# An expert stage whose VectorE order and whose release of one PSUM bank are changed

## The reference

```
def _expert(x, g, b, W1, b1, W2, b2, Wo, bo):     # D = 128, H = 512
    x = _layernorm(x, g, b)
    x1 = x @ W1 + b1
    x2 = jnp.clip(x @ W2 + b2, -20.0, 20.0)
    hidden = jnp.clip(x1 * (x2 * jax.nn.sigmoid(x2)), -10000.0, 10000.0)
    return jnp.clip(hidden @ Wo + bo, -10000.0, 10000.0)
```

## Time and profile before

| | |
|---|---|
| median of 3 runs | 2611.97 us |
| the profiled execution's own time | 2612.07 us |
| its span | 2610.4 us |
| PE busy | 2346.8 us (90%) |
| DVE busy | 2235.7 us (86%) |
| ACT busy | 1657.2 us (63%) |
| POOL busy | 1498.2 us (57%) |
| mean granted TensorE clock | 0.954 |

### The profile page before, as it was taken

The page is one execution under the profiler, slowest core; times in us unless marked ns, Lnnn a source line. Parts: engine busy times, 40 slices in busy tenths (PEclk is TensorE's granted clock), DMA queues, the critical chain, the costliest instruction groups (busy, mean ns, idle before and its releaser), DMA issues. The chain is left out here.

```text
span 2610.4 us, 44164 instructions
## 1 busy us (share of the span) xinstructions
PE 2346.8 (90%) x15048; PEld 1785.9 (68%) x15048; DVE 2235.7 (86%) x4680; ACT 1657.2 (63%) x2873; POOL 1498.2 (57%) x1073
## 2 busy tenths in 40 slices
PE   5995699927999999999999999999999999939994
PEld 3553588715777777777777777777777777628883
DVE  6666477759999999999999999999999999847775
ACT  2464233336777777787877778787778877623333
POOL 0145344415666666667668766666866766734442
PEclk8997799958999999999999999999999999969997
DMA  8721466563454345334422342233323332025555
GB/s 203 212 69 41 139 191 189 153 153 97 98 128 100 89 99 131 92 87 103 97 61 70 84 94 71 61 76 83 95 63 76 77 87 49 14 68 184 187 181 159
DMA packets 171280, 281.11 MB, mean 108 GB/s; under 512 B 33292, under 2 KB 124818, under 8 KB 171056
## 3 DMA queue, kind: packets, MB, share of 16 engines
q1 hardware_dynamic: 161392, 259.31, 38.7%
q0 software_dynamic: 9664, 18.97, 2.1%
HBM read 118.15 MB, written 63.31 MB: 70 GB/s over the span
## 5 line engine op out<-in xcount | busy, mean ns | idle before, releaser
L2334 POOL TENSOR_TENSOR b_prob<-b_prob,b_weight 128x1024 f32<-128x1024 f32 x512 | 958.8, 1904 | 504.5 <-DVE b_weight L2292 503.4
L2262 DVE TENSOR_REDUCE b_bmax<-b_score 128x16 f32<-128x1024 f32 x512 | 620.9, 1213 | 42.5 <-PE b_score L2113 27.4
L2214 ACT ACTIVATE b_prob<-b_score,b_neg_m 128x1024 f32<-128x1024 f32 x512 | 582.1, 1137 | 76.4 <-DVE b_neg_m L2270 74.8
L2249 DVE TENSOR_REDUCE b_bsum<-b_prob 128x16 f32<-128x1024 f32 x512 | 605.6, 1202 | 0.0
L2199 ACT ACTIVATE b_pT<-b_turn 128x512 f32<-128x512 f32 x1024 | 560.9, 609 | 61.6 <-PE b_turn L2126 54.5
L2126 PE MATMUL b_turn<-ident,b_prob 128*128 128x128 f32 x4096 | 531.8, 273 | 4.8 <-ACT b_pT L2199 4.3
L2126 PEld LDWEIGHTS b_turn<-ident,b_prob 128*128 128x128 f32 x4096 | 479.1, 141 | 76.1 <-ACT b_pT L2199 4.4
L2113 PE MATMUL b_score<-b_KH,b_QS 128*128 128x512 f32 x1024 | 478.8, 468 | 16.6 <-ACT b_prob L2214 14.8
L2093 PE MATMUL b_acc<-b_pT,b_V 128*64 128x256 f32 x4096 | 470.3, 382 | 0.0
L2113 PE MATMUL b_score<-b_KL,b_QS 128*128 128x512 f32 x1024 | 405.1, 396 | 0.0
L2093 PEld LDWEIGHTS b_acc<-b_pT,b_V 128*64 128x64 f32 x4096 | 282.4, 137 | 150.9 <-issue 21.2
(11 more groups left out here) (310 smaller groups left out, 2972.2 us busy)
## 6 DMA issues: line engine op xcount, KB each, us to landing
f_e_w<-f_weights SPq DMA_DIRECT2D x78, 776.0 KB
f_sorted<-zeros SPq DMA_DIRECT2D x172, 193.5 KB, 5.2
b_KH<-b_k_high SPq DMA_DIRECT2D x128, 256.0 KB
b_KL<-b_k_low SPq DMA_DIRECT2D x128, 256.0 KB
b_QS<-b_q_high SPq DMA_DIRECT2D x64, 256.0 KB, 3.8
b_QS<-b_q_low SPq DMA_DIRECT2D x64, 256.0 KB, 4.8
b_hb<-b_hT SPq DMA_DIRECT2D x31, 512.0 KB
f_e_z<-f_sorted SPq DMA_DIRECT2D x78, 129.0 KB
```

Source lines behind the costliest of these rows:

```text
L2214: act.activation(prob[r % 4][k][:], score[k % 2][:], ACT.Exp, bias=neg_m[r % 2][:, k:k + 1]).then_inc(prob_ready, 1)
L2249: dve.tensor_reduce(bsum[r % 2][:, k, :], prob[r % 4][k][:].rearrange("p (n c) -> p n c", c=KV_BLOCK), AX, ALU.add).then_inc(sum_ready, 1)
L2262: maxima = chain.mark(dve.tensor_reduce(bmax[r % 2][:, k, :], score[k % 2][:].rearrange("p (n c) -> p n c", c=KV_BLOCK), AX, ALU.max))
L2334: pool.tensor_tensor(tile, tile, weight[r % 2][:, k, :].unsqueeze(2).to_broadcast([P, NB, KV_BLOCK]), ALU.mult).then_inc(scaled, 1)
```

## The change

VectorE's order in a step becomes: product 0, clip 1, finish(t-2), places, clip 2, product 1, clip 3, product 2, clip 0 of block t+1, product 3, clamp_back. So product 0 is put ahead of clip 1, and finish ahead of places. A new semaphore `py_taken` is signalled by the add of `finish`, which reads bank `py`; VectorE waits on it before the clamp of the sum (in place of the wait on the chain), and TensorE's `down` waits on it in place of `y_ready`. The loads and stores still wait on `y_ready`.

```
             if t >= 1:
-                pe.wait_ge(y_ready, blocks_before + t)
+                pe.wait_ge(py_taken, blocks_before + t)
...
-        chain.link(dve.tensor_tensor(y[i][:], py[:, 0:ROWS].rearrange("p (q d) -> p q d", d=D),
-                                     bo[i][:].unsqueeze(1).to_broadcast([P, QB, D]), ALU.add))
+        dve.tensor_tensor(y[i][:], py[:, 0:ROWS].rearrange("p (q d) -> p q d", d=D),
+                          bo[i][:].unsqueeze(1).to_broadcast([P, QB, D]), ALU.add).then_inc(py_taken, 1)
+        dve.wait_ge(py_taken, blocks_before + t + 1)
         dve.tensor_scalar(y[i][:], y[i][:], CLAMP, -CLAMP, ALU.min, ALU.max).then_inc(y_ready, 1)
...
     def step(j, t, i):
         for c in range(HC):
+            if c == 0:
+                product(t, i, c)
             if c < HC - 1:
                 clip_x2(j, t, i, c + 1)
             elif t < BLOCKS - 1:
                 clip_x2(j + (i + 1) // DEEP, t + 1, (i + 1) % DEEP, 0)
-            product(t, i, c)
+            if c:
+                product(t, i, c)
+            if c == 0 and t >= 2:
+                finish(j - (1 if i < 2 else 0), t - 2, (i - 2) % DEEP)
             if c == 0:
                 places(j, t, i)
-            if c == 0 and t >= 2:
-                finish(j - (1 if i < 2 else 0), t - 2, (i - 2) % DEEP)
             if c == HC - 1:
                 clamp_back(t, i)
```

More of the change, by code:

```diff
@@ L1466, in __init__ @@
         self.steps = [sem("e_" + n) for n in ("turned", "zT_ready", "x2_done", "up_done", "x2_ready", "act_ready", "x1_taken",
-                                              "front_ready", "back_ready", "down_done", "y_ready")]
+                                              "front_ready", "back_ready", "down_done", "y_ready", "py_taken")]
         self.loads = [[sem(f"e_{n}{i}") for i in range(self.DEEP)] for n in ("w_loaded", "bo_loaded", "z_loaded")]
@@ L1491, in run_experts @@
         turn, py = bank("turn"), bank("py")
-        turned, zT_ready, x2_done, up_done, x2_ready, act_ready, x1_taken, front_ready, back_ready, down_done, y_ready = sems.steps
+        turned, zT_ready, x2_done, up_done, x2_ready, act_ready, x1_taken, front_ready, back_ready, down_done, y_ready, py_taken = sems.steps
         w_loaded, bo_loaded, z_loaded = sems.loads
```

## The result

The changed kernel takes 2588.97 us (median of 4 runs, 2586.78 to 2590.96) against 2611.2 us before (now the median of 4 runs): a ratio of 0.9917, 95% interval 0.9905 to 0.9929. The prediction was 2590. The profiled execution took 2587.66 us, its span is 2585.7 us, so between the two profiled executions lie 24.4 us.

The account below looks back on a forecast made before the run. TensorE bounds the expert stages, stalled for product 0: 69 x 0.39 = 26.9 us, less 5.3 for late rows, plus 1.2 at stage ends, less 0.8, gives 22.0 us, so 2590; range 2586 to 2602 (8 in 10).

Parts of the forecast that it names:

- The stall of `up(t,3)`: TensorE in each expert block: waiting for product 0 costs 0.39 us; without it a block takes 5.45 instead of 5.84.
- Rival (c): At `up(t,3)` or `down`: another gate holds as long as before, time stays at 2610 to 2612; chance 0.07.
- The store's hold: GpSimd's second indirect store on clamp_back: the clamp starts 0.43 into it, slips through and takes 0.43 us.
- Rival (a): At clamp_back: held every second block, mean block 5.57 us, gain 15 us, 2597; chance 0.20.
- (d): At clamp_back: held in every block until the store ends, 6.0 us a block, 11 us slower, 2623; chance 0.05.
- py_taken: At `down`: release by the add, 0.2 us to spare; nothing alone in regular blocks, without it up to 0.2 lost a block.
- Places behind finish, the chain wait replaced: On VectorE: zero effect for both, within 0.05 either way, all of it under TensorE.
- The transfers: Row and weight loads: 7 late weight loads gain nothing, 8 late row loads cost 5.3 us, just-in-time loads 0.8.
- Rival (b): At row or weight loads: they take the stall's place, blocks of 5.65 us, about 2599; chance 0.18.
- The ends of the stages: Last `down` of each expert stage: 0.6 us gained a stage, bounded by 0.3 and 0.8, 1.2 for both.

Follow-up runs that it names:

- the run with the order alone: Changed kernel with the new VectorE order, but `down` waiting on `y_ready` as before: ratio 0.9986, 2612.27 us against 2615.15.
- product 0 ahead of clamp_back: The kernel with rows first, with product 0 of the next block also put ahead of clamp_back: ratio 0.9867 to the kernel before.
- the order-only kernels with the split clamp: New VectorE order with `down` on `y_ready`, GpSimd's clamp written as two or four instructions: ratios 0.9933 and 0.9946 to the kernel before.
- earlier row loads: Changed kernel with block t+2's row load waiting for product 1 of block t-1, not finish of t-2: ratio 0.9891 to the kernel before.
- the kernel with rows first: Changed kernel with early row loads issued ahead of the weights in each step, and weights in two loads: ratio 0.9857, 2567.72 us against 2604.69.

## Why the prediction was right, step by step

**The stall of `up(t,3)`**, 0.39 us a block: measured 5.84 - 5.46 = 0.38. The wait for the product fell from 34 to 3 in the first stage, and no other engine's wait took its place. Rival (c) is refuted. The path was right as far as it went: TensorE did wait for product 0. But product 0 was late behind a held clamp as well as behind clip 1, and by the sum of the rows it was the hold's cycle of 5.84 us that set the block before; the prediction has the hold of 0.09 and not the cycle.

**The store's hold** on clamp_back: forecast 0.43 after the store's start, and passing. It was at 0.42 to 0.43 in 29 of the 72 intervals, and took 0.43 us in 61; the other 11 were held, and in ten of them clamp_back comes at U+1.78 in place of U+1.68. The changed kernel narrows where the hold begins. Two of its blocks, each with its second store and clamp_back:

```profile
458.22 1.06 POOL L1635 DMA_INDIRECT f_outputs<-f_e_y,f_e_dest  x1 [0.30 <-issue]
458.73 0.43 DVE L1692 TENSOR_SCALAR f_e_hT<-f_e_hid 128x512 f32<-128x512 f32 x1
...
401.43 0.98 POOL L1635 DMA_INDIRECT f_outputs<-f_e_y,f_e_dest  x1 [0.30 <-issue]
...
401.96 0.70 DVE L1692 TENSOR_SCALAR f_e_hT<-f_e_hid 128x512 f32<-128x512 f32 x1
```

At 0.51 the clamp passed, and the store took 1.06 in place of 0.98 us: this time the store waited. Its record ends 0.12 after the clamp's end, and so it does for all seven clamps of this kernel that started 0.45 to 0.51 into it (stores of 1.00 to 1.06 us). At 0.53 the clamp was held and ended 1.23 after the store's start; at 0.52 it was held in the kernel before. Rival (a) is refuted as a rule for every second block, and (d) by the clamps at 0.42, 0.43 and 0.51: a hold from under 0.25 to the store's end would have caught all of them. The Trainium skill's rule ("SBUF — State Buffer", "Who interferes with whom"), that the first gets the pair and the other fully blocks, holds in both directions here, but for a part of the store's record, not all of it.

**py_taken**: the down product needs it, as I said, but I priced its absence at "up to 0.2 us a block", and the run with the order alone lost 0.38. Two terms were off. A release by the add or the clamp of the sum reaches the weight load 0.12 after its modelled end, and I had counted 0.05, from the product. And I had worked out the hold for the changed kernel only; 0.16 us more in a block moved the clamp from 0.42 to 0.57. The steady state that I described for rival (d) exists, 0.22 deep in the kernel with the order alone and 0.09 deep in the kernel before. The alternation of rival (a) exists too: in the changed kernel the block held at 0.53 took 5.68 us, and the next clamp came 0.27 after its store and passed. The difference is the length of a held block. A held clamp puts the next second store 5.84 behind its own. A held block of the order-only kernel also takes 5.84, so the next clamp meets its store at the same place; one of 5.68 brings the next clamp nearer to its store's start, and out of the hold.

**Places behind finish, the chain wait replaced**, taken at zero: no run has either by itself. The room for them can be read from the others. The add's release comes at U+3.40 in the changed kernel; a release at U+3.60 cost 0.03 us a block (product 0 ahead of clamp_back), one at U+3.73 cost 0.16 (the order-only kernels with the split clamp), so `down`'s load wants it by U+3.57. There are 0.17 us of room, where 0.2 was forecast, and `places` takes up 0.07 of VectorE's time. Zero is an estimate from these rows.

**The transfers**: taken at 8.8 us: 2.7 for seven blocks with late weights (76 x 0.39 less 69 x 0.39), 5.3 for late rows and 0.8 for loads just in time. The 72 intervals lie 8.9 above 72 x 5.845 before and 14.3 above 72 x 5.46 after, so 5.4 us of the gain were lost, the changed kernel's held clamps among them. The term was 3.4 us too large. The split among them was not as I had it: the second stage lost most to the weights, up to 2.2 us at once. Rival (b) was there in part: 10 row waits of 5.6 us in both stages, which earlier row loads removed but for 0.2 us. That the lateness is one of when and in what order loads are issued, not of traffic, is shown by the kernel with rows first: it moves the same bytes in less time and has none. Issue time and order changed together there, so which of the two counts for more stays open.

**The ends of the stages**: forecast 0.6 each beside the last block's 0.39, so 2.0 us for both stages. From the start of block 38 to the first of the last two stores it was 523.83 - 512.50 = 11.33 us before, and is 506.51 - 495.79 = 10.72 after: 0.6 for the end and the last block together, and as much in the second stage. The new release gives 0.33 of it and not the 0.45 that I took: the last `down` now starts 0.12 after the add's end where it started 0.12 after the clamp's. Another 0.2 is luck: the last clamp of the sum took 0.50 us before, inside a store, and takes 0.29 after. The last block is led by VectorE (its add stands behind product 3 and clamp_back, which the first store holds), so its TensorE gain did not come through.

The sum: 22.4 us in the 72 intervals, 1.2 at the ends and 0.8 that I did not trace further (the first blocks are outside the intervals), together the 24.4 between the profiled executions; 22.0 was forecast, and 22.2 lies between the medians. The mechanism was right, but that the forecast comes within 0.2 us of the medians is partly luck: lateness cost 3.4 us less than forecast, the last blocks gave 0.8 less, and the two profiled executions alone would put the forecast 2.4 too low.

## What to carry to other kernels

Two small edits can be worth next to nothing apart and 0.8% together, when each uncovers the other's wait and only both bring the period out of a cycle that another pair of engines holds: after an edit, ask what is late next by a tenth of a microsecond before calling it useless. Where two engines share a port, a period that changes by 0.16 us can move an instruction into the other engine's hold, and the hold can keep itself in place; check where it falls for each version, not for one, and when two versions have exactly the same period, look for the cycle that they share. When a compute stall is gone, look at the load queue: when each load is issued, and whether a small urgent one can go ahead of a large patient one.

## What the runs showed of the hardware that I had not expected

An indirect store on GpSimd (0.98 us in the record) keeps an SBUF-to-SBUF VectorE operation out from between 0.51 and 0.52 to about 0.80 after its start. One that starts at 0.51 or before passes, and where it ends later than about 0.86 into the store, the store ends 0.12 after it (1.06 us for the clamp at 0.51). For the first store of a pair (1.02 us in the record) the beginning is near 0.53: in the order-only kernel with two instructions one clamp at 0.53 was held (0.74 us) and one at 0.53 passed (the store took 1.08). Operations that read PSUM ran through such stores at their usual 0.47 and 0.54 us.

Splitting a GpSimd clamp of 128 x 512 into two of 128 x 256 changed it from one record of 0.61 us to two of 0.39, 0.36 to 0.37 apart, and the kernel around it became 0.5% faster: slower work on an engine with time to spare moved its next instruction out of the way.
